# A graph attention layer on one core: low parts in pairs on VectorE, preparation work moved to GpSimd, jobs moved to other steps

## What is computed

```python
h  = relu(layernorm(x))
hs = layer_norm(h) ; ht = layer_norm(h_target)          # scale, bias, node mask
q = (ht @ Wq + bq) / sqrt(32) ; k = hs @ Wk + bk ; v = hs @ Wv + bv
logits = where(adj != 0, q @ k.T, -1e30)                 # per head, 2048 x 2048
ctx = softmax(logits) @ v
ht = layer_norm(ht + ctx @ Wo + bo)
y  = x + ht + gelu(ht @ W1) @ W2
```

## Time and profile before

| | us |
|---|---|
| median of 3 runs | 711.27 (708.77 to 711.74) |
| the profiled execution, its own time | 710.3 |
| its span (what the trace covers) | 708.5 |
| PE / DVE / POOL / ACT busy | 660.1 / 591.8 / 520.9 / 455.1 |

### The profile page before, as it was taken

One profiled execution on the slowest core, in us unless ns is written; L12 is line 12 of the kernel. 1 busy time (PEld: TensorE's weight loads), 2 busy tenths in 40 slices (PEclk: granted clock), 3 DMA queues, 4 the chain that ended last, 5 costly groups with the idle time before them and its releaser, 6 DMA issues. The chain is left out here.

```text
span 708.5 us, 20214 instructions
## 1 busy us (share of the span) xinstructions
PE 660.1 (93%) x8326; PEld 470.7 (66%) x8326; DVE 591.8 (84%) x972; ACT 455.1 (64%) x811; POOL 520.9 (74%) x495
## 2 busy tenths in 40 slices
PE   4996899999999999999999999999999899898998
PEld 4563566766776677667767766777677667456667
DVE  5996799989999989999999799989978897564661
ACT  4742566766776658677766686777666788756550
POOL 3620879889999966889999677999977777370430
PEclk9999999999999999999999999999999999999999
DMA  8735411113001020120001112021000000000001
GB/s 297 260 75 176 134 31 59 34 62 105 2 2 32 19 74 29 56 83 2 4 31 41 52 32 76 17 70 53 2 2 2 2 2 2 1 1 31 16 23 52
DMA packets 20795, 36.20 MB, mean 51 GB/s; under 512 B 2752, under 2 KB 13280, under 8 KB 20704
## 3 DMA queue, kind: packets, MB, share of 16 engines
q1 hardware_dynamic: 20704, 34.92, 15.8%
HBM read 26.49 MB, written 2.10 MB: 40 GB/s over the span
## 5 line engine op out<-in xcount | busy, mean ns | idle before, releaser
L1333 POOL TENSOR_TENSOR prob_lo<-prob 128x512 f16<-128x512 f32 x380 | 439.0, 1179 | 95.4 <-ACT prob L838 93.7
L838 ACT ACTIVATE prob<-score 128x512 f32<-128x512 f32 x512 | 305.0, 597 | 164.1 <-PE score L440 156.4
L440 PE MATMUL early<-kT,qT 96*128 96x512 f16 x512 | 192.2, 380 | 20.2 <-DVE half_max L1123 19.3
L440 PE MATMUL score<-nidentb,mask_nat 128*128 128x128 bf16 x2048 | 199.0, 220 | 2.9 <-ACT prob L838 1.6
L440 PE MATMUL score<-qT,kT 97*128 97x512 f16 x512 | 196.3, 383 | 0.0
L440 PEld LDWEIGHTS ctx<-v_sb,prob 128*128 128x128 bf16 x2048 | 159.1, 98 | 54.1 <-ACT raw L860 9.4
L440 PE MATMUL ctx<-v_sb,prob 128*128 128x65 f16 x2048 | 191.4, 193 | 0.6 <-POOL prob_lo L1333 0.5
L440 PE MATMUL ctx<-v_sb,prob_lo 128*128 128x65 f16 x2048 | 190.4, 193 | 0.0
L1123 DVE CUSTOM_DVE_ANT_0 early<-early,mask_nat,half_max 128x1024 f32<-128x1024 f32 x128 | 163.5, 1284 | 24.5 <-PE early L440 24.0
L1123 DVE CUSTOM_DVE_ANT_0 early<-early,mask_nat 128x1024 f32<-128x1024 f32 x128 | 156.8, 1228 | 23.2 <-PE early L440 21.2
L440 PEld LDWEIGHTS ctx<-v_sb,prob_lo 128*128 128x128 f16 x2048 | 142.7, 97 | 49.9 <-issue 4.0
(11 more groups left out here) (162 smaller groups left out, 597.2 us busy)
## 6 DMA issues: line engine op xcount, KB each, us to landing
adj_in<-in_adj SPq DMA_DIRECT2D x26, 512.0 KB, 3.9
qT<-q_stage SPq DMA_DIRECT2D x48, 64.0 KB, 2.0
kT<-mask_nat SPq DMA_DIRECT2D x48, 64.0 KB, 2.0
raw<-in_x SPq DMA_DIRECT2D x4, 512.0 KB, 5.6
tgt<-in_L_gnn_h_target SPq DMA_DIRECT2D x4, 512.0 KB, 11.4
prob<-in_adj SPq DMA_DIRECT2D x4, 512.0 KB, 10.2
nT<-in_L_gnn_W SPq DMA_DIRECT2D x2, 1024.0 KB, 6.8
mask_nat<-in_x SPq DMA_DIRECT2D x1, 2048.0 KB, 9.0
```

The lines of the kernel that those rows point to most:

```text
L440: return nc.tensor.matmul(dst, w, m, start=start, stop=stop, **more)
L838: nc.scalar.activation(prob[:, n % SLOTS, :], score[n % 2][:, :], ACT.Exp).then_inc(exp_done, 1)
L1333: nc.gpsimd.tensor_tensor(prob_lo[:, n % SLOTS, :], prob[:, n % SLOTS, :], prob_hi(n % SLOTS), ALU.subtract).then_inc(lo_sem["pool"], 1)
```

## The change

1. DVE takes the low parts of two neighbouring tiles by one operation of 128 x 1024 (`low_parts_of`), which waits for the second one's exponential: tiles (12, 13) in unit 0, (4, 5) and (12, 13) in units 1 to 29, every second pair in units 30 and 31. That is 1 + 29 x 2 + 2 x 4 = 67 operations for 134 tiles.
2. Low parts of value blocks 3 to 7 go to POOL: ACT first copies the bank in full to SBUF (`v_full`, 2 buffers), then makes the high part from the copy; PE waits for the copy alone.
3. The feature sums go to POOL, as six foldings in halves (`fold_features`), interleaved with its value low parts; one reduction stays on DVE, behind `maxima(8)`.
4. Twelve early pairs ahead of unit 0's loop (FILL = 4 more), and two a j only for j = 0, 1; the products of the mean come after the first five scores.
5. Tables: masks, context norms, sums, CT_AT and WO_AT at other steps.
6. Tail: second `turn_context` one place later, `out_row`s one place later, and results 0 and 1 of block 0 between the four `lead_stats`.
7. ACT: features of the last group and one high part ahead of two deviations and the table load; DVE: one `target_stats` behind two low parts.

```diff
+FILL = 4
+V_DVE = 3
-CT_AT = {(2, 1): 0, (2, 4): 1}
-WO_AT = {(2, 11): 0, (3, 1): 1}
+CT_AT = {(2, 6): 0, (2, 11): 1}
+WO_AT = {(2, 13): 0, (3, 1): 1}
-MASK_DVE = [(0, 6), (2, 1), (2, 4), (2, 7), (3, 7), (4, 3), (4, 7), (5, 3)]
+MASK_DVE = [(0, 6), (2, 4), (2, 6), (3, 2), (3, 7), (4, 3), (4, 7), (5, 3)]
-SUM_AT = [(0, 3), (0, 11), (1, 1), (1, 7)]
-NORM_AT = [(0, 5), (1, 1), (1, 3), (1, 5)]
+SUM_AT = [(0, 3), (0, 11), (1, 5), (2, 1)]
+NORM_AT = [(0, 5), (1, 1), (1, 5), (2, 2)]
-DVE_LO = [()] + [(2, 6, 10, 14)] * (UNITS - 3) + [tuple(range(1, STEPS, 2))] * 2
+DVE_LO = [(12,)] + [(4, 12)] * (UNITS - 3) + [tuple(range(2, STEPS, 4))] * 2
 def pairs_at(u, j):
     if u == 0:
-        first = RAMP + (2 * j if j < 6 else j + 6)
-        return range(first, first + (2 if j < 6 else 1))
+        first = RAMP + FILL + (2 * j if j < 2 else j + 2)
+        return range(first, first + (2 if j < 2 else 1))
...
 # PE
-                for e in range(TT, RAMP):
+                for e in range(TT, RAMP + 2):
                     for i in range(2):
                         early_scores(e, i)
-                    if e == RAMP - 2:
-                        mean_values()
                 shift_row(0)
                 for n in range(AHEAD):
                     scores(n)
+                    if n in (1, 3):
+                        for i in range(2):
+                            early_scores(RAMP + 2 + n // 2, i)
+                mean_values()
...
-                    if f in (5, 6):
-                        turn_context(NTB - 1, f - 5)
+                    if f in (5, 7):
+                        turn_context(NTB - 1, f // 2 - 2)
...
-                    if f in (1, 3):
-                        for t in (f - 1, f):
+                    if f in (2, 4):
+                        for t in (f - 2, f - 1):
                             out_row(NTB - 1, t)
...
 # ACT
                 def high_values(i):
                     act.wait_ge(v_ready, i + 1)
+                    if i >= V_DVE:
+                        if i >= V_DVE + 2:
+                            act.wait_ge(v_lo_pool, i - V_DVE - 1)
+                        nc.scalar.activation(v_full[:, i % 2, :], value_bank(i), ACT.Copy).then_inc(v_out, 1)
+                        act.wait_ge(v_out, i - V_DVE + 1)
...
 # DVE
-                def low_part(n):
-                    dve.wait_ge(exp_done, n + 1)
-                    nc.vector.tensor_tensor(prob_lo[:, n % SLOTS, :], prob[:, n % SLOTS, :], prob_hi(n % SLOTS),
-                                            ALU.subtract).then_inc(lo_sem["dve"], 1)
+                def low_parts_of(n):
+                    dve.wait_ge(exp_done, n + 2)
+                    two = slice(n % SLOTS, n % SLOTS + 2)
+                    nc.vector.tensor_tensor(prob_lo[:, two, :], prob[:, two, :], prob_his(two), ALU.subtract).then_inc(lo_sem["dve"], 1)
...
+                for e in range(TT, RAMP + 1):
+                    maxima(e)
+                dve.wait_ge(folded, 6)
+                nc.vector.tensor_reduce(feat_all[:, :], fold[:, 0, :, 0:TB // 8], AX, ALU.add).then_inc(feat_done, 1)
+                for e in range(RAMP + 1, RAMP + FILL):
                     maxima(e)
                 mean_low()
...
                 for t in range(TT):
+                    if t % 2 == 0:
+                        result(0, t // 2)
                     lead_stats(NTB - 1, t, t == TT - 1)
                 lead_scale(NTB - 1, lead_width(NTB - 1))
-                results(0)
+                for t in range(2, TT):
+                    result(0, t)
...
 # POOL
+                def fold_features(i):
+                    if i < 2:
+                        pool.wait_ge(nT_masked, DC * (2 * i + 2))
+                        if i == 0:
+                            pool.wait_ge(tp_ready, DC * len(GROUPS))
+                        dst, a, b = fold[:, i, :, :], nT[:, 2 * i, :, :], nT[:, 2 * i + 1, :, :]
+                    else:
+                        pool.wait_ge(folded, i)
+                        half = TB >> (i - 2)
+                        dst, a, b = fold[:, 0, :, 0:half], fold[:, 0, :, 0:half], fold[:, 0, :, half:2 * half] if i > 2 else fold[:, 1, :, :]
+                    nc.gpsimd.tensor_tensor(dst, a, b, ALU.add).then_inc(folded, 1)
...
+                fold_features(0)
+                for i in range(V_DVE, NT // 2):
+                    low_values(i)
+                    fold_features(i - V_DVE + 1)
```

More of the change, by code:

```diff
@@ L125, in lo_counts @@
     for n in range(TILES):
-        who = "dve" if n % STEPS in DVE_LO[n // STEPS] else "pool"
-        count[who] += 1
+        who = "dve" if n % STEPS // 2 * 2 in DVE_LO[n // STEPS] else "pool"
+        count[who] += 1 if who == "pool" or n % 2 == 0 else 0
         done.append((who, count[who]))
@@ L138, in lo_here @@
     soon = range(u * STEPS + 2 * j + 3, u * STEPS + 2 * j + 5)
-    return [n for n in [*first, *soon] if n < TILES and LO_DONE[n][0] == "dve"]
+    return [n for n in [*first, *soon] if n < TILES and LO_DONE[n][0] == "dve" and n % 2 == 0]
 def adj_use(k, i):
@@ L301, in prob_hi, with prob_his @@
             return prob[:, slot, :].bitcast(BF16).rearrange("p (t two) -> p t two", two=2)[:, :, 1]
+        def prob_his(slots):
+            return prob[:, slots, :].bitcast(BF16).rearrange("p b (t two) -> p b t two", two=2)[:, :, :, 1]
         def proj_bank(g, m):
@@ L310, in value_bank, with value_read @@
                 return early[1][:, i * TB:(i + 1) * TB]
-            return (score if i < 4 else (ctx, aux))[i % 2][:, :]
+            return ((ctx, aux) if i in (4, 5) else score)[i % 2][:, :]
+        def value_read(eng, i):
+            if i < V_DVE:
+                eng.wait_ge(v_lo, i + 1)
+            else:
+                eng.wait_ge(v_out, i - V_DVE + 1)
         def raw_of(k):
@@ L1209, in _ @@
                 low_values(0)
-                for k in range(1, 3):
-                    target_stats(k)
+                target_stats(1)
                 low_parts(2)
+                target_stats(2)
                 low_values(1)
@@ L1245, in _ @@
                         for n in lo_here(u, j):
-                            low_part(n)
+                            low_parts_of(n)
                         for e in pairs_at(u, j):
@@ L1283, in shifted_rows, with result @@
                                                        in1=xin[:, n, :], op0=ALU.mult, op1=ALU.add).then_inc(t1_done, 1)
+                def result(k, t):
+                    n = k * TT + t
+                    dve.wait_ge(r_done, n + 1)
+                    dve.wait_ge(down_ready, n + 1)
+                    if n >= 4:
+                        dve.wait_ge(stored[n % 4], n // 4 * 16)
+                    nc.vector.scalar_tensor_tensor(out=yout[:, n % 4, :], in0=row[n % 2], scalar=node_f[:, n:n + 1],
+                                                   in1=xin[:, n, :], op0=ALU.mult, op1=ALU.add).then_inc(y_done, 1)
                 def results(k):
                     for t in range(TT):
[L1287 to L1293 removed]
+                        result(k, t)
                 denominators(NTB - 1)
@@ L1399, in _ @@
                     for m in range(STEPS):
-                        if m not in DVE_LO[u]:
+                        if m // 2 * 2 not in DVE_LO[u]:
                             low_part(u * STEPS + m)
```

60 lines of the change are left out of this document (25 added, 35 removed).

## The result

The changed kernel takes **716.83 us** (median of 6 runs, 714.68 to 718.41), the one before 710.1 (6 runs, 708.77 to 711.74): a ratio of 1.0088, with a 95% interval of 1.0066 to 1.011. It is slower by 6.7 us, where 702.4 was forecast. The profiled executions have spans of 714.9 and 708.5.

| stretch | before | after | change | forecast |
|---|---|---|---|---|
| to the start of unit 2 | 105.3 | 108.8 | +3.5 | -3.7 |
| units 2 to 31 | 496.5 | 503.8 | +7.3 | -0.6 |
| behind the last exponential | 106.8 | 102.3 | -4.5 | -5.1 and +0.5 |
| of the span, at a granted clock of 0.50 | 6.8 | 17.0 | +10.2 | 0 |

A forecast was written before the change was run, and what follows sets the result against it. PE, busy 93% of the span, was taken as the bound, then its waits for DVE's maxima. Front 3.7 + loop 0.6 - unit 31's last pair 0.5 + tail 5.1 = 8.9 off 710.3: 701.4, as median 702.4; range 693 to 709.

The forecast's parts named there:

- ACT's five extra copies and POOL's 11 us of foldings and low parts lie beside this.: Ahead of the loop: this work, about 50 to 62 us, runs alongside; the eighth maxima come 4.6 us earlier, at 62.1.
- Now it comes to them at 84.9 ... 91.5.: Unit 0: SP reaches the adj pieces at 84.9, DVE's mask waits for them, early pair 23 comes at 91.5, gaining 5.1.
- I take 0.8: Unit 1: the half-clock stretch after PE's idling costs 0.8 us, of up to 1.7.
- The pair: DVE's 128 x 1024 low-part operation takes 1.23 us plus a wait w; DVE's time per unit falls by 1.0 us.
- w: A pair's wait for POOL's running operation, taken as 0.2 us; whatever exceeds 0.31 stalls PE, 3 us over 60 pairs.
- The slower rival: Loop: each pair waits for nearly a whole POOL operation, 0.84 us, giving 720; chance 0.06.
- The loop: Units 2 to 31: 6 gained, less 4.5 at `turn_context` and 0.9 at `out_row`, leaves 0.6 us gained, between -6 and +9.
- Removed stalls: Units 2 to 31: 9 of PE's stalls go, 3 come back through pairs that wait too long, net 6 us gained.
- Which covers it: Loop: exponentials run five tiles ahead, some 3.9 us, so six POOL tiles in a row don't make PE wait.
- The tail: Behind the loop: 2.1 us gained at the second transpose and 3.0 at `down_products`; unit 31's last pair loses 0.5.
- the lump eats it: Rival for the loop: w stays at 0.28, 8 us of new stalls, about 711, no change; chance 0.10.
- The mask does not gate: Rival: the front gains 8 to 10 instead of 3.7, or short waits let the loop give 6 to 9; 696; chance 0.24.

The follow-up runs named there:

- e7: The changed kernel with SP's queue reordered as in e2 and POOL's first folding held until DVE has made the masks of block 0: 709.64 us, ratio 0.9974.
- e2: The changed kernel with SP placing copies of groups 2 and 3 ahead of the weights, which wait for the second folding instead of `feat_done`: 713.68 us.
- e12: e9 with two useless PE products of 128 x 512 behind each of five early pairs ahead of the loop: 700.27 us, ratio 0.9838.
- e9: Kernel before with the changed front and tail, single low parts, old tables, SP's order of e2 and the folding wait of e7: 702.69 us.
- e8: The changed kernel with the last context norm moved to (1, 7) and its sum to (1, 9): 713.91 us, ratio 1.0024.
- e3: The changed kernel with the five tables of the kernel before (CT_AT, WO_AT, MASK_DVE, SUM_AT, NORM_AT): 713.07 us, ratio 1.0012.
- e10: The kernel before with DVE's low parts in pairs and nothing else changed, a rerun for a trace: 716.93 us, ratio 1.0083.
- e5: The changed kernel with DVE's low parts single as before (tiles 2, 6, 10, 14): 716.69 us, ratio 1.0069.
- e11: e9 with pairs of low parts, and all masks but the first at j = 1 or 5, one j behind a pair: 695.96 us, ratio 0.9782.
- e4: The kernel before with the changed tail alone: 706.18 us, ratio 0.9918.
- e13: e11 with the useless products of e12: 694.14 us, ratio 0.9752.

## Why the prediction was wrong

The forecast was -8.9 us, the result +6.7 (+6.4 by the traces). Its steps in turn:

1. **"ACT's five extra copies and POOL's 11 us of foldings and low parts lie beside this."** This step failed first. For the low parts behind 50 us it held; the first folding came at 42.2, beside DVE's last masks of block 0, which my sum had left out. It made of a mask of 0.68 (e7) one of 2.82. The eighth maxima came 3.3 late (65.4 for 62.1), and `feat_done` 3.7 late, as it also waited 0.22 for POOL's last folding. With the folding held back (e7) 1.9 and 1.8 of these go; the other 1.4 us of the maxima was missing from the sum as well, 0.86 of it a wait of PE for the masks.
2. **"Now it comes to them at 84.9 ... 91.5."** The mechanism was right and shown by e2; the sizes were 89.65 and 97.40. Of the 5.9 us by which pair 23 missed its forecast, 3.7 come from step 1, 1.1 from SP's copies (22.4 for 21.3) and 1.0 from the landing (94.84 less 89.65 is 5.2, for 4.2). The range's lower end for the front, +2, left no place for a loss.
3. **"I take 0.8" for the clock.** A wrong size. I took one stretch of 3.4 us to come in unit 1 and one to go in the tail: 6.8 us as before, where 17.0 stand, and 10.2 more than before ahead of unit 2. At the 0.37 of e12 these 10.2 are an estimated 3.7, but what of it lay before pair 23 was covered by the wait for the piece of adj. From pair 23 to the start of unit 2 it was 11.4 us for 8.7: +2.7, where 0.6 + 0.8 was forecast. e12 shows it from the other side: with PE kept busy no half clock is left in its span, and it takes 2.4 us less than e9. The 3.4 us in unit 28 cost next to nothing (e8).
4. **The pair.** 1.23 was right (median 1.226), w = 0.2 nearly so (1.469 - 1.226 = 0.24). But the mean was the wrong thing to ask: of the 63 pairs in units 2 to 31, 43 wait 0.31 or less and 13 wait over 0.7, nearly a whole operation of POOL. The excess over 0.31 is 8.5 us in all, where "60 pairs with a mean excess of w over 0.31 of 0.05: 3" stands. The slower rival, in which each pair waits so, did not happen; a fifth of them do. In e3, where three pairs wait 0.88 that do not in e10, each costs PE 0.9 us (below); what the 8.5 cost in after was not measured by itself.
5. **The loop.** This step failed with the first, and costs as much: forecast -0.6, measured +7.3. Removed stalls: forecast -6, counted -6.2. `turn_context` +4.5: +5.1. `out_row` +0.9: +0.7. What was missing is what I had put at nothing or not named: scores, which wait for exponentials (+2.2), contexts, which wait for POOL (+2.2), and `shift` (+1.1). The waits of the scores come with the pairs (3.0 us in after, e3 and e10 alike, 1.6 in e5 and before). "Which covers it", of the six tiles in a row on POOL, did not hold everywhere. And the -6 itself should have been more: the text saw the lump at (2, 4) and overlooked the four masks that stand right ahead of a pair. Against e3, which has the same pairs and the masks of before (five of them right ahead of a pair), e11 with none takes 12.0 us less in the loop. The wait of `turn_context` was no plain loss either: taken away in e8, nearly half of it came back as other waits.
6. **The tail.** Forecast -5.1 and +0.5, measured -4.5; alone, in e4, -5.2. Right, with the mechanism: the waits of 2.66 and 2.96 are gone.

Of the rivals, "the lump eats it" (0.10) was nearest for the loop, with the clock and the front on top. "The mask does not gate" (0.24) fell. The chance of 0.06 for slower hung on one mechanism alone, and it was slower mainly by others.

One more comparison: units 2 to 31 take 501.7 us in e3 and 499.2 in e10, with the same tables and pairs. All of it lies in units 10, 18 and 26, 0.9 in each (17.8, 17.2, 17.2 for 16.9, 16.3, 16.3), and just ahead of each stands one pair that takes 2.09, 2.10 and 2.08 us in e3 and 1.21 three times in e10. The first of the three, POOL and DVE, in e3 and then in e10:

```profile
238.65 1.04 POOL L1356 TENSOR_TENSOR prob_lo<-prob 128x512 f16<-128x512 f32 x1 [0.17 <-ACT prob L863]
238.68 2.09 DVE L1154 TENSOR_TENSOR prob_lo<-prob 128x1024 f16<-128x1024 f32 x1
...
237.37 2.13 POOL L1336 TENSOR_TENSOR prob_lo<-prob 128x512 f16<-128x512 f32 x1 [0.19 <-ACT prob L841]
237.38 1.21 DVE L1135 TENSOR_TENSOR prob_lo<-prob 128x1024 f16<-128x1024 f32 x1
```

Both begin within 0.03 us of each other; in e3 DVE is the one held up, in e10 POOL. What tips it, and how a changed front comes to shift it, stays open.

## What to carry to other kernels

Long operations of an engine that works in order must be placed apart: two in a row (mask and pair, 3.4 us) lose what halving their number gives, and with six table entries moved the loop took 489.7 us (e11) for 501.7 (e3). Price an operation that another engine can hold up by its cases as well as by its mean: the pair's 1.47 hides 40 of at most 1.3 us and 19 of over 1.7. Work given to an engine "that has time" is to be laid beside what the others do at that very moment: a folding of 2.72 us on POOL stopped DVE, PE, SP's queue and a DMA in turn. And a wait of PE can be paid twice, where the clock falls behind it (2.5 us in e9) and others don't wait in its stead (unit 28); where PE must wait, useless products can be cheaper than idling.

## What the runs showed of the hardware

**POOL holds up DVE's masks.** One mask, 128 x 1024 from int32, took 2.82 us beside a folding that had begun 0.45 before it, and 0.68 with the folding held back (e7). It ended 0.55 after the folding did (42.67 + 2.82 = 45.49; 42.22 + 2.72 = 44.94), as if it had only begun then. The Trainium skill (SBUF — State Buffer, Who interferes with whom) says this: a `tensor_scalar` of VectorE can run in a mode that takes the port shared with GpSimd, and whoever issues first holds it for the whole instruction while the other is blocked. This trace agrees. The same rule was weighed in the prediction for the pairs alone, where the trace of before was said to show it in part only.

**The price of being held up.** The other masks of the loop go by the same sum in both kernels: what is left of POOL's operation when they begin, and 0.55 (0.77 left: 1.32; 0.96 left: 1.51; 0.40 left: 0.95), or 0.69 where nothing or little (0.08) is left. So do DVE's pairs in after: what is left, and 1.09 (0.98 left: 2.07; 0.77: 1.85; 0.40: 1.48; 0.19: 1.28), or 1.19 to 1.23 beside none. Two of 37 took longer (1.84 and 1.85), where another operation of POOL, of 0.73 us, followed at once. The other way round, a low part of POOL that begins during a pair mostly ends 0.90 us after the pair does: begun 0.42 after the pair it took 1.70, for 1.04 alone.

**The clock.** After a wait of 1.78 us and little before it (0.86 of 2.5 us busy) it stood at 0.50 for 3.4 us (e10), after one of 3.71 for 6.8 (after). A wait alone does not tell: behind one of 2.95 us at 46.5 it fell in e2, behind one of 2.89 at 46.3 it stayed up in after. The stretches of the kernels read here last 3.4, 6.8 or, in e7, 10.2 us. In the loop they stand in unit 28 (563.9 in after, 559.6 in e2, 556.6 in e7, 556.7 in e10, 541.6 in e11) or in unit 3 (e3, e10); the other kernels have none there, e13 among them, whose useless products lie 480 us earlier. What decides it was not looked into.
